# A retention block between two quantized FFNs: VectorE's first chains alternated, chunk 5's first FFN before V 0, and steps 2 and 3 in another order

## The chip, the cores and the metric

One Trainium2 chip, eight cores, one batch element per core: every core runs the same program on its own X of 2048 x 1024, with its own copy of all weights. The metric is the device time of the slowest core in microseconds.

## What is computed

For each X (fp32), with H = 8 heads of DH = 128:

```python
x = x + 0.5 * ffn(layernorm(x), W, b)      # "f1"
x = x + attn(layernorm(x))                 # retention: k q g v, sc, ret, wo
x = x + 0.5 * ffn(layernorm(x), W, b)      # "f2", the same W and b
# ffn: x and W quantized in blocks of 32 to the FP6 E2M3 grid, scaled back, x @ W.T + b
# attn: scores q k^T / sqrt(DH), causal, decayed by gamma_h^(n-m), times v;
#       normalised per head; silu(x @ W_G) * that, @ W_O
```

## The kernel before, in words

The sequence is cut into 16 chunks of 128 rows (partitions). For every chunk c the program runs: layernorm statistics (`st1` on VectorE, small terms `sm1` on GpSimd), the centred copy `xc1` (ScalarE), quantization `q1` on VectorE (a maximum over blocks of 32, a scale, a reciprocal, a multiply that writes fp8; it counts semaphore v_q1), scaling back `xd1` and the addition of the bias `b1` (GpSimd), a transpose of xd1, the matmuls `f1` and their addition into x, `ev1` (VectorE). Then `st2`, `sm2`, the normalised t (`tn`, ScalarE), its transpose, four projections `proj` k, q, g, v of 16 matmuls of 128 x 512 each, which are emptied by `evK`, `evQ`, `evG` (ScalarE) and `evV` (VectorE); the scores `sc`, `mask` (VectorE), `ret` with the update of the running state, `gn` statistics (VectorE), `smG` (GpSimd), `norm` (ScalarE), `zmul` (VectorE), the transpose of z, `wo`, `evO`. Then the second FFN with `st3`, `sm3`, `xc2`, `q2`, `xd2`, `b2`, `f2`, `ev2`, and a store.

At the start the FFN's weight is quantized in 8 blocks of 128 rows: `wquant` (lines 413 to 428, four steps, VectorE), `wy8` (rounding to fp8, ScalarE), `wd` (scaling back, GpSimd), a transpose `wtr` on TensorE and its copy `wcp` out of PSUM (ScalarE). A step on VectorE that needs the result of the step before waits for a semaphore of its own engine (`step`, line 409). The other weights come by `cast_load` (line 1039), fp32 to bf16, two halves each, issued from GpSimd. wg and wo have their place where the FFN's weight was staged, so they are loaded only when its blocks are through. Everything else is loaded by SyncE (`x_first`, line 280), which also issues the transposes by DMA: `xdt1` from chunk 6 on, `tt` from 3, `kt` and `qt` from 1, `zt`, `xdt2` (lines 293 to 333). The earlier ones go over TensorE (`turn`, line 903) and a copy on ScalarE (`turned`, line 706).

Each engine works through a list written out by hand: SyncE's is at lines 351 to 403, VectorE's at 534 to 635, ScalarE's at 723 to 811, TensorE's at 935 to 1029, GpSimd's at 1115 to 1207. The first four "steps" are irregular, and from chunk 4 (STEADY) on a loop repeats one pattern, in which f1 is three chunks ahead of the projections and f2 three behind. In each list an instruction that waits holds all behind it.

The matmuls write into three pairs of PSUM banks, P0 to P2; P1 also holds sc and ret. `psum_users` (line 86) lists, in TensorE's order, which work takes which pair, and `emptied` (line 824) makes each wait for the emptying of the last one: `EMPTIED`, line 120. v_sb, z_sb, st_sb, kt_sb and qt_sb are single buffers; `kt(c)` waits for the scores of c-1, `qt(c)` for ret of c-1, `evV(c)` for the state update of c-1.

Of the kernel before, what the change touches and what calls it, by code (L numbers as in the profile page):

```python
# [124 lines left out]
def build_program():  # L125
# [280 lines left out]
    def prog_vector(e):  # L406
# [126 lines left out]

        wquant(0)
        wquant(1)
        st1(0)
        for j in range(2, 6):
            wquant(j)
        q1(0)
        wquant(6)  # L540
        st1(1)
# [731 lines left out]
```

## Time and profile before

| | |
|---|---|
| Median of 3 runs | 484.29 us (484.23 to 484.36) |
| The profiled execution | 484.67 us, of which the slowest core's span is 482.8 us |
| The other cores' spans | 479.5 to 481.6 us |
| TensorE busy | 432.3 us (90%) |
| VectorE, ScalarE, GpSimd busy | 342.6, 190.5, 256.4 us |
| The chain that ended last | TensorE 72%, VectorE 12%, issue 6%, ScalarE 3%, DMA 3% |
| DMA engines' busy share, first tenths of the span (0 to 108 us) | 0.7, then 0.9 and more, until about 100 us |
| The last multiply of the weight's quantization ends | 40.9 us |
| x of 512 KB, median from issue to landing | 5.3 us |
| A halved weight by cast load, median to landing | wk 19.9, wq 31.5, wg 40.0, wv 41.2, wo 34.0 us |

Times in the rows are microseconds from the span's start of the slowest core. A busy share is the time in which an engine worked; matmuls are pipelined, so a busy TensorE is not at its peak. An idle time in brackets stands before the instruction and names what released it. What matters in this kernel is where TensorE stands idle, and which engine's list it then waits for.

### The profile page before, as it was taken

The page shows a single profiled execution, that of the slowest core. Times are in us where ns is not written, and L with a number is a line of the kernel's source. Part 1 is how long each engine was busy: PE and PEld are TensorE (multiplying, and loading weights), DVE is VectorE, ACT ScalarE, POOL GpSimd, SP SyncE. Part 2 cuts the span into 40 slices and gives each one's busy share as a digit, 9 for nine tenths or more (in the row PEclk, how much of TensorE's full clock was granted, in tenths as well). Part 3 has the DMA queues.
Part 4 walks back from the last instruction along what each step waited for, and adds up shares of the span by engine and source line. Part 5 has one row for each costly group of instructions (what it writes and reads, how often), then busy time and mean ns, then how long its engine had stood idle before and what let it go on. Part 6 is the DMA issues. An engine that isn't in the chain of part 4 may idle for free.

```text
span 482.8 us, 8182 instructions; the slowest of 8 cores (479.5 to 482.8 us)
## 1 busy us (share of the span) xinstructions
PE 432.3 (90%) x2410; PEld 215.5 (45%) x2456; DVE 342.6 (71%) x656; ACT 190.5 (39%) x270; POOL 256.4 (53%) x328
## 2 busy tenths in 40 slices
PE   0226799999998999999999999999999999999894
PEld 0113354545543535454545445454545454555442
DVE  3886866477888859687786868586947466756782
ACT  1547265236442071607061533426152534614400
POOL 0888765325477554655647464647451624436243
PEclk9999899999999999999999999999999999999999
DMA  7999999974363393635343533645340524233143
GB/s 200 309 182 182 189 157 183 155 116 87 89 110 67 94 208 92 110 67 143 75 133 67 153 68 88 88 88 88 87 81 12 107 45 85 47 67 65 44 153 131
DMA packets 99451, 54.47 MB, mean 113 GB/s; under 512 B 88784, under 2 KB 89040, under 8 KB 99408
## 3 DMA queue, kind: packets, MB, share of 16 engines
q1 hardware_dynamic: 93984, 43.43, 39.5%
q0 software_dynamic: 5280, 10.49, 14.9%
q8 instruction: 20, 0.33, 0.3%
q14 instruction: 23, 0.19, 0.1%
q10 hardware_dynamic: 144, 0.03, 0.0%
HBM read 34.28 MB, written 8.39 MB: 88 GB/s over the span
## 4 chain that ended last, share of the span: by engine, by line
PE 72%; DVE 12%; issue 6%; ACT 3%; DMA 3%; POOL 2%; SPq 1%; DVEq 1%; ACTq 0%; POOLq 0%
PE p L818 64%; DVE p L419 2%; DVE arena L434 2%; PE p L928 2%; DMA arena<-arena 2%; PE pstate L908 1%; PE p L859 1%; DVE arena L444 1%; DMA arena<-wf 1%; PE p L863 1%; PE p L847 1%; ACT arena L709 1%; ACT arena L681 1%; PE pstate L872 1%; DVE arena L522 1%
## 5 line engine op out<-in xcount | busy, mean ns | idle before, releaser
L818 PE MATMUL p<-arena 128*128 128x512 bf16 x1715 | 383.2, 379 | 8.1 <-ACT arena L709 2.7
L818 PEld LDWEIGHTS p<-arena 128*128 128x128 bf16 x1760 | 169.6, 98 | 206.8 <-issue 10.6
L434 DVE BATCH_NORM_STATS2 arena<-arena 128x6 f32<-128x512 f32 x96 | 66.5, 692 | 9.9 <-DVE arena L436 2.2
L669 ACT ACTIVATE arena<-arena 128x1024 bf16<-128x1024 f32 x16 | 19.9, 1243 | 129.1 <-POOL arena L1072 129.1
L1112 POOL TENSOR_TENSOR arena<-arena 128x1024 bf16<-128x1024 fp8e4 x16 | 34.3, 2144 | 46.9 <-DVE arena L449 46.9
L681 ACT ACTIVATE arena<-p,arena 128x128 bf16<-128x128 f32 x128 | 46.4, 473 | 19.2 <-POOL arena L1085 19.2
L444 DVE TENSOR_REDUCE arena<-arena 128x32 f32<-128x1024 f32 x29 | 35.3, 1216 | 19.3 <-ACT arena L660 10.8
L513 DVE TENSOR_TENSOR arena<-p,arena 128x1024 bf16<-128x1024 f32 x16 | 19.6, 1223 | 41.0 <-PE p L818 40.5
L908 PE MATMUL pstate<-arena 128*128 128x128 bf16 x168 | 16.4, 261 | 34.3 <-POOL arena L1048 27.5
L1105 POOL TENSOR_TENSOR arena<-arena 128x1024 bf16<-128x1024 fp8e4 x16 | 30.5, 1909 | 29.3 <-DVE arena L449 26.3
L449 DVE SCALAR_TENSOR_TENSOR arena<-arena 128x1024 fp8e4<-128x1024 f32 x29 | 37.3, 1285 | 3.4 <-DVE arena L448 0.5
L1091 POOL TENSOR_TENSOR arena<-arena 128x1024 f32<-128x1024 f32 x16 | 37.6, 2350 | 3.3 <-ACT arena L653 3.3
L1096 POOL TENSOR_TENSOR arena<-arena 128x1024 f32<-128x1024 f32 x16 | 37.5, 2346 | 0.0
L1052 POOL TENSOR_SCALAR arena<-arena 128x1 f32<-128x1 f32 x48 | 10.7, 224 | 44.6 <-DVE arena L436 43.1
L1082 POOL TENSOR_SCALAR arena<-arena 128x8 f32<-128x8 f32 x16 | 4.0, 250 | 53.8 <-DVE arena L526 53.8
L689 ACT CAST arena<-p 128x1024 bf16<-128x1024 f32 x16 | 16.2, 1014 | 41.1 <-PE p L818 41.1
L908 PEld LDWEIGHTS pstate<-arena 128*128 128x128 bf16 x168 | 13.5, 118 | 39.5 <-issue 38.4
L1053 POOL TENSOR_TENSOR arena<-arena 128x1 f32<-128x1 f32 x48 | 27.3, 570 | 7.1
L709 ACT COPY arena<-pstate 128x1024 bf16<-128x1024 bf16 x21 | 20.9, 1009 | 21.4 <-PE pstate L908 19.0
L503 DVE TENSOR_TENSOR arena<-p,arena 128x1024 bf16<-128x1024 f32 x16 | 19.5, 1220 | 13.2 <-PE p L847 12.9
L522 DVE BATCH_NORM_STATS2 arena<-p 128x6 f32<-128x128 f32 x128 | 26.8, 282 | 2.3 <-PE p L859 2.0
L1084 POOL TENSOR_TENSOR arena<-arena 128x8 f32<-128x8 f32 x16 | 26.8, 1676 | 2.3
(52 smaller groups left out, 397.1 us busy)
## 6 DMA issues: line engine op xcount, KB each, us to landing
arena<-x SPq DMA_DIRECT2D x16, 512.0 KB, 5.3
out<-arena SPq DMA_DIRECT2D x16, 512.0 KB, 2.8
arena<-wf SPq DMA_DIRECT2D x8, 512.0 KB, 11.5
arena<-wk POOLq DMA_DIRECT2D x2, 1024.0 KB, 19.9
arena<-wq POOLq DMA_DIRECT2D x2, 1024.0 KB, 31.5
arena<-wg POOLq DMA_DIRECT2D x2, 1024.0 KB, 40.0
arena<-wv POOLq DMA_DIRECT2D x2, 1024.0 KB, 41.2
arena<-wo POOLq DMA_DIRECT2D x2, 1024.0 KB, 34.0
```

The costliest lines, as they stand in the source:

```text
L434: step(e.bn_stats(bn_ln[:, n, 6 * half:6 * half + 6], x[:, 512 * half:512 * half + 512]))
L444: step(e.tensor_reduce(amax.unsqueeze(2), b32(xc), AX, ALU.max, apply_absolute_value=True))
L449: e.scalar_tensor_tensor(b32(y8), b32(xc), sm[:, n, c, 2:3], bc32(rs), ALU.mult, ALU.mult, saturate=False).then_inc(sem[done], 1)
L522: own.up(e.bn_stats(bn_gn[:, h, :], P1[:, h * 128:(h + 1) * 128]))
L681: e.activation(z_sb[:, h * 128:(h + 1) * 128], P1[:, h * 128:(h + 1) * 128], AF.Identity, scale=gn_a[:, h:h + 1], bias=gn_nb[:, h:h + 1]). ...
L818: last = e.matmul(pair[:, half * 512:half * 512 + 512], lhs[:, kc, :], w[:, kc, half * 512:half * 512 + 512], start=(kc == 0), stop=(kc == ...
L908: last = e.transpose(tb[n % 2][:, kc * 128:(kc + 1) * 128], src[:, kc * 128:(kc + 1) * 128], id_sb)
L1053: step(e.tensor_tensor(sm[:, n, c, 0:1], sm[:, n, c, 3:4], nhalf[:, 0:1], ALU.pow))
L1091: e.tensor_tensor(x_sb[c % XR], x_sb[c % XR], bias_sb, ALU.add).then_inc(sem["g_b1"], 1)
L1096: e.tensor_tensor(x_sb[c % XR], x_sb[c % XR], bias_sb, ALU.add).then_inc(sem["g_b2"], 1)
L1105: e.tensor_tensor(b32(xd1_sb[c % 2]), b32(y81_sb[c % 2]), bc32(q1_scl[c % 2]), ALU.mult).then_inc(sem["g_xd1"], 1)
L1112: e.tensor_tensor(b32(xd2_sb), b32(y82_sb), bc32(q2_scl), ALU.mult).then_inc(sem["g_xd2"], 1)
```

## The change

It touches the lists of all five engines and the list of PSUM users.

- VectorE: `wquant` and the first three `q1` and `st1` are split into single steps (w_max, w_scale, w_recip, w_mul; x_max, x_scale, x_recip, x_mul; x_st for each half, x_mean). They stand interleaved, so that most steps wait for one that lies two or more instructions back. The waits are on the count that its own forerunner reached. After them, st1(5) stands before q1(4), ev1(5) before evV(0), st2(3) before st1(6), evV(2) right behind gn(1), st1(7) behind st3(0).
- ScalarE: a small activation into `warm` before the first wy8, behind the same wait for g_const; wy8(1) before xc1(0); xc1(2) before wcp(7); xc1(5) before tn(2); xcp(5) before evG(1); xc1(6) behind evG(2) and evK(2) before norm(0); xc1(7) behind xc2(0), evQ(3) before scopy(2).
- TensorE: f1(1) in halves with the turn of x2 between them; xtr(5) before proj(1, "g"); f1(5) before proj(0, "v") instead of behind ret(0); proj(2, "g") before sc(1) and proj(2, "v") before ret(1); proj(3, "k") before f1(6) and proj(3, "q") before ret(2).
- GpSimd: the loads of wg's second half and wv's first are issued behind sm1(2); xd1(2) before b1(1); wv's second half behind sm2(0); sm1(5) before b1(4); sm2(3) before sm1(6); sm1(7) behind sm3(0).
- SyncE: kt(1) and qt(1) before the load of chunk 6, which waited for k 1; the load of chunk 7 waits for wv; kt(2) before zt(0); qt(3) before xdt2(0).

```diff
-             ("g", 1, 1), ("v", 0, 0), ("sc", 0, 1), ("v", 1, 2), ("ret", 0, 1),
-             ("f1", 5, 0), ("k", 2, 2), ("q", 2, 0), ("sc", 1, 1), ("g", 2, 2),
-             ("ret", 1, 1), ("wo", 0, 0), ("v", 2, 2),
-             ("f1", 6, 0), ("sc", 2, 1), ("k", 3, 2), ("ret", 2, 1), ("wo", 1, 0),
-             ("q", 3, 2), ("g", 3, 0), ("f2", 0, 2), ("v", 3, 1)]
+             ("g", 1, 1), ("f1", 5, 0), ("v", 0, 2), ("sc", 0, 1), ("v", 1, 0),
+             ("ret", 0, 1), ("k", 2, 2), ("q", 2, 0), ("g", 2, 2), ("sc", 1, 1),
+             ("v", 2, 0), ("ret", 1, 1), ("wo", 0, 2),
+             ("k", 3, 0), ("f1", 6, 2), ("sc", 2, 1), ("q", 3, 0), ("ret", 2, 1),
+             ("wo", 1, 2), ("g", 3, 0), ("f2", 0, 2), ("v", 3, 1)]
...
# SyncE
-        e.wait_ge(sem["t_k"], 2)
+
+        kt(1)
+        qt(1)
         x_first(6)
 
-        kt(1)
+        e.wait_ge(sem["ld_wv"], 32)
         x_first(7)
-        qt(1)
+        kt(2)
         zt(0)
         tt(3)
-        kt(2)
         qt(2)
...
         kt(3)
+        qt(3)
         xdt2(0)
         x_first(9)
-        qt(3)
...
# VectorE
+        def w_scale(j):
             if j >= 4:
                 e.wait_ge(sem["g_wd"], j - 3)
...
+            e.wait_ge(sem["v_self"], at["w_max", j])
+
+            own.up(e.tensor_scalar(w_scl[j % 4], w_amax[j % 4], 0.5 * R7_5, 0.5 * FLOOR,
+                                   ALU.mult, ALU.max))
+            at["w_scale", j] = own.n
...
+        w_max(0)
+        w_scale(0)
+        w_max(1)
+        w_recip(0)
+        w_scale(1)
+        w_mul(0)
+        x_st(0, 0)
+        w_recip(1)
+        x_st(0, 1)
+        w_mul(1)
+        w_max(2)
+        x_mean(0)
+        w_scale(2)
+        for j in range(3, 6):
+            w_max(j)
+            w_recip(j - 1)
+            w_scale(j)
+            w_mul(j - 1)
+        x_max(0)
+        w_recip(5)
+        x_scale(0)
+        w_mul(5)
+        w_max(6)
+        x_recip(0)
+        w_scale(6)
+        x_mul(0)
+        x_st(1, 0)
+        w_recip(6)
+        x_st(1, 1)
+        w_mul(6)
+        w_max(7)
+        x_mean(1)
+        w_scale(7)
+        x_st(2, 0)
+        w_recip(7)
+        w_mul(7)
+        x_max(1)
+        x_st(2, 1)
+        x_scale(1)
+        x_mean(2)
+        x_recip(1)
+        x_mul(1)
+        x_max(2)
+        x_scale(2)
+        x_recip(2)
+        x_mul(2)
...
         st1(4)
+        st1(5)
         q1(4)
         ev1(3)
-        st1(5)
         q1(5)
         ev1(4)
+        ev1(5)
         evV(0)
         mask(0)
 
         gn(0)
         evV(1)
+
+        st2(3)
         st1(6)
-
-        ev1(5)
-        st2(3)
         zmul(0)
         mask(1)
         q1(6)
-        st1(7)
         gn(1)
+        evV(2)
         evO(0)
         st3(0)
-        evV(2)
+        st1(7)
         zmul(1)
...
# TensorE
         f1_half(0, 1)
-        f1(1)
+        f1_half(1, 0)
         xtr(2)
+        f1_half(1, 1)
         f1_half(2, 0)
...
         f1(4)
+        xtr(5)
         proj(1, "g")
-        xtr(5)
         e.wait_ge(sem["s_t"], 3)
         turn("t2", t_sb)
+        f1(5)
         proj(0, "v")
 
         sc(0)
         proj(1, "v")
         ret(0)
 
-        f1(5)
         proj(2, "k")
         proj(2, "q")
+        proj(2, "g")
         sc(1)
-        proj(2, "g")
+        proj(2, "v")
         ret(1)
         wo(0)
-        proj(2, "v")
-
+
+        proj(3, "k")
         f1(6)
         sc(2)
-        proj(3, "k")
+        proj(3, "q")
         ret(2)
         wo(1)
-        proj(3, "q")
         proj(3, "g")
...
# GpSimd
         cast_load("wg", 0)
         wd(5)
-        cast_load("wg", 1)
         xd1(0)
         b1(0)
         wd(6)
-        cast_load("wv", 0)
         sm1(1)
         wd(7)
         xd1(1)
         sm1(2)
+        cast_load("wg", 1)
+        cast_load("wv", 0)
+        xd1(2)
         b1(1)
+        sm2(0)
         cast_load("wv", 1)
-        xd1(2)
-        sm2(0)
         b1(2)
```

ScalarE's part of the diff is told in the list above.

## Rows read from the trace of the kernel before

**Rows 1.** Table of windows: length, busy (instructions) of each engine, clock, DMA share, GB/s.

```profile
130.00:190.00 60.00, 56.77 (x321) 27.84 (x326) 50.15 (x92) 19.95 (x30) 36.08 (x43) 1.00 0.54 110
...
190.00:250.00 60.00, 59.69 (x321) 29.16 (x326) 46.65 (x103) 24.52 (x36) 33.41 (x49) 1.00 0.50 111
```

**Rows 2.** Timeline, VectorE, one weight block: start, duration, line, shapes.

```profile
15.60 1.23 DVE L419 TENSOR_REDUCE p<-arena 128x32 f32<-128x1024 f32 x1 [0.17 <-DVE arena L436]
...
16.93 0.19 DVE L422 TENSOR_SCALAR arena<-p 128x32 f32<-128x32 f32 x1
...
17.23 0.36 DVE L424 RECIPROCAL p<-arena 128x32 f32<-128x32 f32 x1
...
17.76 1.22 DVE L427 SCALAR_TENSOR_TENSOR arena<-arena,p 128x1024 f32<-128x1024 f32 x1 [0.17 <-DVE p L424]
...
18.90 1.22 DVE L419 TENSOR_REDUCE p<-arena 128x32 f32<-128x1024 f32 x1
```

**Rows 3.** Chain that ended last, 48 to 60 us: start, duration, what.

```profile
48.46 1.24 DVE p L444
...
50.69 1.29 DVE arena L449
...
52.19 1.91 POOL arena L1105
...
56.30 2.94 PE p L928 x8
...
59.24 0.85 PE pstate L908 x8
```

**Rows 4.** Timeline, GpSimd: sm1(2)'s first instruction, and b1(1).

```profile
46.63 0.21 POOL L1052 TENSOR_SCALAR arena<-arena 128x1 f32<-128x1 f32 x1
...
48.28 2.36 POOL L1091 TENSOR_TENSOR arena<-arena 128x1024 f32<-128x1024 f32 x1
```

**Rows 5.** Timeline, TensorE: sc(0), three projections, sc(1).

```profile
96.13 0.61 PE L847 MATMUL p<-arena 128*128 128x128 bf16 x8
...
101.14 10.36 PE L818 MATMUL p<-arena 128*128 128x512 bf16 x47
...
111.34 0.61 PE L847 MATMUL p<-arena 128*128 128x128 bf16 x8
```

**Rows 6.** DMA issues: KB each, us to landing; issued at 25.65, 32.24, 50.57, 98.23.

```profile
arena<-wq POOLq DMA_DIRECT2D x1, 1024.0 KB, 34.3
...
arena<-wg POOLq DMA_DIRECT2D x1, 1024.0 KB, 41.9
...
arena<-wv POOLq DMA_DIRECT2D x1, 1024.0 KB, 39.2
...
arena<-x SPq DMA_DIRECT2D x1, 512.0 KB, 6.2
```

**Rows 7.** Timeline: gn(0) to evV(1), q1(6) to st1(7) on VectorE; a ScalarE pass.

```profile
100.75 1.68 DVE L522 BATCH_NORM_STATS2 arena<-p 128x6 f32<-128x128 f32 x8 [1.99 <-PE p L859]
...
103.10 1.19 DVE L513 TENSOR_TENSOR arena<-p,arena 128x1024 bf16<-128x1024 f32 x1
...
113.27 1.21 DVE L444 TENSOR_REDUCE arena<-arena 128x32 f32<-128x1024 f32 x1
...
116.66 1.48 DVE L434 BATCH_NORM_STATS2 arena<-arena 128x6 f32<-128x512 f32 x2
...
118.60 1.15 ACT L653 ACTIVATE arena<-arena 128x1024 f32<-128x1024 f32 x1 [0.55 <-DVE arena L436]
```

**Rows 8.** Chain that ended last, 129 to 156 us.

```profile
129.11 1.21 DVE arena L503
...
137.18 1.12 DVE arena L484
...
150.91 4.70 DMA arena<-arena
...
155.84 2.32 PE p L818 x10
```

More of the change, by code:

```diff
@@ new lines, in x_max, with x_scale @@
+        def x_max(c):
+            e.wait_ge(sem["s_xc1"], c + 1)
+            own.up(e.tensor_reduce(x_amax[c].unsqueeze(2), b32(xc1_sb[c % 2]), AX, ALU.max,
+                                   apply_absolute_value=True))
+            at["x_max", c] = own.n
+        def x_scale(c):
+            e.wait_ge(sem["g_sm1"], c + 1)
+            if c >= 2:
+                e.wait_ge(sem["g_xd1"], c - 1)
+            e.wait_ge(sem["v_self"], at["x_max", c])
+            own.up(e.tensor_scalar(q1_scl[c % 2], x_amax[c], sm[:, 0, c, 1:2], FLOOR,
+                                   ALU.mult, ALU.max))
+            at["x_scale", c] = own.n
@@ new lines, in x_recip, with x_mul, x_st @@
+        def x_recip(c):
+            e.wait_ge(sem["v_self"], at["x_scale", c])
+            own.up(e.reciprocal(x_rs[c], q1_scl[c % 2]))
+            at["x_recip", c] = own.n
+        def x_mul(c):
+            e.wait_ge(sem["v_self"], at["x_recip", c])
+            e.scalar_tensor_tensor(b32(y81_sb[c % 2]), b32(xc1_sb[c % 2]),
+                                   sm[:, 0, c, 2:3], bc32(x_rs[c]), ALU.mult, ALU.mult,
+                                   saturate=False).then_inc(sem["v_q1"], 1)
+        def x_st(c, half):
+            if c >= 1 and half == 0:
+                e.wait_ge(sem["v_st1"], c)
+            e.wait_ge(sem["ld_x%d" % c], 16)
+            own.up(e.bn_stats(bn_ln[:, 0, 6 * half:6 * half + 6],
+                              x_sb[c][:, 512 * half:512 * half + 512]))
+            at["x_st", c] = own.n
@@ L531, in zmul @@
             e.tensor_tensor(z_sb, z_sb, g_sb[c % 2], ALU.mult).then_inc(sem["v_z"], 1)
[L534 to L541, printed above, removed]
-        wquant(7)
-        q1(1)
-        st1(2)
-        q1(2)
+        w_max(0)
[44 more added lines that the diff above has]
+        x_mul(2)
         ev1(0)
@@ L723, in prog_scalar @@
         e.dma_start(out=id_sb, in_=id_dr).then_inc(sem["ld_ident"], 16)
-        for j in range(KC - 1):
-            wy8(j)
-            if 2 <= j:
-                wcp(j - 2)
-            if j == 2:
-                xc1(0)
-            if j == 4:
-                e.wait_ge(sem["ld_bias"], 16)
-                e.activation(bias_sb, bias_sb, AF.Identity, scale=0.5
-                             ).then_inc(sem["s_bias"], 1)
-        xc1(1)
+        e.wait_ge(sem["g_const"], 2)
+        e.activation(warm, nhalf, AF.Identity, bias=ntie)
+        wy8(0)
+        wy8(1)
+        xc1(0)
+        for j in range(2, 6):
+            wy8(j)
+            wcp(j - 2)
+        e.wait_ge(sem["ld_bias"], 16)
+        e.activation(bias_sb, bias_sb, AF.Identity, scale=0.5).then_inc(sem["s_bias"], 1)
+        wcp(4)
+        wy8(6)
         wcp(5)
         xcp(0)
+        xc1(1)
         wy8(7)
         wcp(6)
+        xc1(2)
         wcp(7)
-        xc1(2)
         xcp(1)
@@ L754, in prog_scalar @@
         turned("q0", qt_sb)
+        xc1(5)
         tn(2)
@@ L766, in prog_scalar @@
         scopy(0)
+        evK(2)
         norm(0)
+        evQ(2)
+        tn(3)
+        evG(2)
         xc1(6)
-        evK(2)
-        tn(3)
-        evQ(2)
-        evG(2)
         scopy(1)
+        norm(1)
+        evK(3)
+        xc2(0)
         xc1(7)
-        norm(1)
-        xc2(0)
-        evK(3)
+        evQ(3)
         scopy(2)
-        evQ(3)
         norm(2)
@@ L1146, in prog_gpsimd @@
         sm2(1)
+        xd1(3)
         cast_load("wo", 0)
-        xd1(3)
+        b1(3)
         cast_load("wo", 1)
-        b1(3)
         sm1(4)
         sm2(2)
+        sm1(5)
         b1(4)
         xd1(4)
-        sm1(5)
         b1(5)
@@ L1159, in prog_gpsimd @@
         smG(0)
+        sm2(3)
         sm1(6)
         b1(6)
-        sm2(3)
         xd1(6)
-        sm1(7)
         smG(1)
         sm3(0)
+        sm1(7)
         b1(7)
```

43 lines of the change are left out of this document (23 added, 20 removed).

## The prediction

> **What bounds the kernel now.** I read the table of windows first, then the timeline of the start, then the chain of waits. From about 190 us on TensorE is full [rows 1]: its list of matmuls is the same in both kernels, so the change can only move the moment at which that gapless stretch begins. Between 130 and 190 us TensorE is idle for 3.2 us [rows 1], and the chain of waits says why: it runs over VectorE from the mask of chunk 2 (129.11) to the transposing DMA that feeds f2(1), where TensorE stands for 1.55 us at 155.84 [rows 8]. The next such point, f2(2) near 184 us, hangs on the same engine's list: ev2(1), gn(3), st2, st3. So there are two limits one behind the other: up to about 125 us the start (VectorE's quantization, then TensorE), from there to 184 us VectorE's list. In the start, VectorE works without a real pause, and in dependent pairs: each of the four steps of a weight block waits for the one before [rows 2]. The last of its products that TensorE needs is y8 of chunk 2 (50.69), from which xd1, the turn and f1(2) follow [rows 3].
>
> **VectorE's alternating chains.** One weight block takes 3.30 us from reduce to reduce: 1.33 + 0.30 + 0.53 + 1.14 [rows 2]. The last step, multiply to the next block's reduce, needs no result of its forerunner, and there the next instruction starts 0.08 us before the 1.22 us are over; at the dependent steps it starts 0.10 to 0.18 after. Alternated (reduce j, reciprocal j-1, scale j, multiply j-1) I get 1.15 + 0.28 + 0.18 + 1.14 = 2.75 us, 0.55 less. I stepped the new list through from 7.15 us with these intervals, and ScalarE and GpSimd beside it: multiply 0 ends at 11.4, multiply 2 at 18.3, 5 at 26.5, chunk 0's y8 at 29.4, multiply 7 at 35.7, where it ends at 40.9 now. GpSimd does not bind before: a block costs it 1.91 and an issue of a cast load 0.8, together 2.7 us, the same pace. ScalarE's table load goes off the path, but multiply 0 is 0.96 later since reduce 1 stands before it: 0.3 us gained.
> From here others set the pace. Chunk 1: xc1(1) ends at 36.2, its y8 at 40.3; GpSimd does wd(7) to 40.0, xd1(1) to 42.4, and only then sm1(2), 1.65 us [rows 4], to 44.1. Chunk 2's scale waits for that; multiply at 45.0, against 50.69 [rows 3]: 5.7 us earlier. xd1(2) goes in front of b1(1), turn at 48.5.
> The skill speaks against this part. The Trainium skill, VectorE: DVE Perf Modes, section "The DRAIN you can't avoid", says that the next operation starts when the pipe is empty and that a semaphore after each adds nothing; by it, alternation would save nothing. The trace disagrees: 1.14 against 1.33 us behind instructions of 1.22 [rows 2].
>
> **TensorE up to sc(0).** f1_half(0,1) and f1_half(1,0) fit in front of the turn of x2. f1_half(1,1) then covers ScalarE's copy, which stands open today until 56.30 [rows 3]. f1_half(2,0) took 2.94 us [rows 3]; eight matmuls at the later rate (0.217 each, [rows 5]) take 1.74. I take the faster for three of the four halves and the slow one where the 1.6 us before x2's turn hide it; if all run slow it costs 1 to 2 us. The next wait is t0: ev1(0) 46.7, st2(0) to 49.8, on GpSimd b1(1), 2.36 [rows 4], to 50.7, sm2(0) to 52.1, tn(0) to 53.5, turn at 53.6 where 59.04 is now (the first of the two turns that rows 3 merge at 59.24). After k 0 the turn of t1 waits another 0.7 us, since sm1(3) and b1(2) stand before sm2(1). Now from 59.04 to sc(0) at 96.13 [rows 5] are 37.1 us; less 0.4 for a wait before x4's turn and 0.6 for slow matmuls, plus the new wait 0.7, plus f1(5), 16 x 0.217 = 3.5. New sc(0): 53.6 + 40.3 = 93.9, call it 94.1. Against the same work now (96.13 + 3.5) it is 5.5 us earlier.
>
> **Loads.** The cast loads of the weights are one queue with a backlog: wg's second half lands 41.9 us after its issue at 32.2, wv's 39.2 after 50.6 [rows 6], so these two, with one load between them, land at 74.1 and 89.8, 7.8 apart each, though they were issued 18.4 apart. Issuing wg 1 at 44 instead leaves two loads before it unfinished, so I price it at nothing, and the landings stay. q 0 wants wq at 60.5 and it lands at 60.0 (34.3 after 25.7 [rows 6]); g 0 wants wg at 76.0, v 0 wants wv at 90.6. None waits, by 0.5, 1.9 and 0.8 us; chunk 5's earlier load shares the engines with the first, so up to 1 us stands against me there. That f1(5) stands before v 0 is what makes the second hold; without it v 0 would be ready at 87.1 and wait 2.7. Chunk 6's load now waits for kt(1) and qt(1): issued at 99.9 instead of 73.8. The load issued at 98.2 took 6.2 us [rows 6]; so 106, and st1(6) begins then rather than at 105. VectorE has 1.5 us to spare there. Bounds: nothing, and 1.5 us if it takes 9.
>
> **Step 2.** v 1, ret(0) with its state update, k 2, q 2, g 2: sc(1) at 109.4 (now 111.34 without g 2 [rows 5]; like for like 5.4 earlier). gn(0) takes 2.35 [rows 7], evV(1) is done at 102.1 before q 2 at 102.5. The queue of SyncE: kt(2) stands before zt(0) and waits for sc(1), so z 0's transpose starts at 111.1 and lands 3 to 4.7 later, wo(0) wants it at 114.6: 0 to 0.9, hidden by the next wait. On ScalarE xc1(6) is now behind evG(2): two passes, 1.15 us for the longer [rows 7], to 111.6. From there VectorE: q1(6) 3.39 [rows 7], gn(1) 2.35, evV(2) 1.2, end 118.7. k 3 takes the PSUM pair of v 2 and waits for evV(2): it starts at 118.8 instead of 118.2. k 3, f1(6): sc(2) at 125.8, mask(2) at 126.35. Now it is at 129.11 [rows 8]: 2.75 us earlier. So of 5.4 us half is given back, in the chain evG(2), xc1(6), q1(6), gn(1), evV(2), k 3, and because k 3 and f1(6) now both stand before sc(2).
>
> **Step 3 and the rest.** Behind mask(2) VectorE's list is unchanged: ev1(6), q2(0), gn(2) (ret(2) is over at 130.6, in time), evO(1). wo(1) ends at 134.5, so evO(1) starts at 134.6 against 137.18 [rows 8]: 2.5 left. st3(1), q1(7), zmul(2), q2(1) follow at their old pace, f2(1)'s transpose lands at 153.1 and f2(1) starts there. TensorE would be ready for f1(7) at 144.8 and stands 2.7 us for the transpose of xd1(7) and 1.9 before f2(1) instead: that is where its lead goes. qt(3) before xdt2(0) waits until 131 and hides no later than xd2(0) does. From f2(1) to f2(2) near 184 everything is VectorE's, ScalarE's and SyncE's old order, and behind it TensorE is full; tail and loads are the same. Sum: 2.5 us off the profiled execution, 484.67 to 482.2. The median of the runs lies 0.4 below that execution, at 484.29, so **481.8 us**.
>
> **Rivals.**
> (A) The forecast, 481.8, with 480.6 to 483.0 for 1 us either way in step 2.
> (B) The lead is kept. Were VectorE's list behind 129 us elastic (the gaps there are waits on a late TensorE, such as 1.4 us before zmul(1)), f2(1) would follow TensorE. For it: mask(2) is gated by sc(2). Against it: gn(2) to q2(1) stand back to back. A f2(1) right behind f1(7) and sc(3), at 148.8, would give 7 us; half of what lies between is 4.7: 479.6.
> (C) The start gains, the middle does not: the x6 load takes 9 us, the first halves run slow, or a weight lands 2 us late at q 0, g 0 or v 0. Each takes 1 to 2 us of the 2.5: 483.3 to 484.5, no change that can be told.
> (D) Slower. The new steps 2 and 3 pay only if sc(0) comes early: the path from sc(0) to mask(2) is 32.3 us, against 33.0 now with f1(5) in it (3.5), so 2.8 longer of its own, k 3 being in it. From sc(0) later than 96.8 mask(2) comes later than 129.1. If alternation saved nothing, multiply 7 stays at 41.7, chunk 2's y8 at 51, sc(0) at 99.6, mask(2) at 131.9: 2.8 us slower, 487.1. For it: nothing in the trace, where the small steps may yet have a floor that 1.14 does not show; half of the saving lost gives 484.4. This is also what the rule named above makes of it.
> A late cast load belongs here as a lesser form: if wg 1 landed 42 us after its issue instead of by its place in the queue, g 0 would wait 10 us. The even spacing speaks against it.
>
> **Chances.** A 0.56, B 0.14, C 0.19, D 0.11. Within 0.2% is within 1 us, which is about what a measurement of this kernel can tell from no change. Faster is A, B and a third of C: 0.77; same is most of C and a little of D: 0.13; slower 0.10. The range takes B and C in: 479.4 to 484.8.
>
> **What would show it.** Multiply to multiply of the weight blocks 2.75 us; y8 of chunk 2 at 45; turn of t0 near 53.6; sc(0) near 94; sc(1) near 109.4; mask(2) near 126.4; TensorE idle between 144 and 154 for 3 us or more in all; f2(1) near 153.3. A mask(2) at 129 or later, TensorE waiting on a cast load, or f2(1) before 152 makes it wrong.

## The result, and the profile after

| | before | after |
|---|---|---|
| Median of 4 runs each, one job | 484.26 us (484.20 to 484.36) | 487.21 us (486.87 to 487.45) |
| Ratio, 95% interval | | 1.0057 (1.004 to 1.0074) |
| Spans of the cores | 479.5 to 482.8 | 481.8 to 485.2 |

The change makes the kernel 2.9 us slower. Forecast were 481.8 us, a range up to 484.8 and a chance of 0.10 for slower: it was wrong. In some executions of the experiments below one die ran at a lower clock and some per cent longer; medians and ratios here leave these out.

The alternation itself does what it should. Timeline of VectorE, kernel after, core 3, beside [rows 2]:

```profile
16.28 1.22 DVE L421 TENSOR_REDUCE p<-arena 128x32 f32<-128x1024 f32 x1
17.41 0.35 DVE L436 RECIPROCAL p<-arena 128x32 f32<-128x32 f32 x1
17.67 0.17 DVE L430 TENSOR_SCALAR arena<-p 128x32 f32<-128x32 f32 x1
17.87 1.22 DVE L443 SCALAR_TENSOR_TENSOR arena<-arena,p 128x1024 f32<-128x1024 f32 x1
19.00 1.22 DVE L421 TENSOR_REDUCE p<-arena 128x32 f32<-128x1024 f32 x1
```

Reduce to reduce is 2.72 us where it was 3.30. The Trainium skill, VectorE: DVE Perf Modes, section "The DRAIN you can't avoid", says that the next operation does not start before the pipe is empty, and the prediction took from it that alternation would save nothing. But the same paragraph goes on to say that a next operation that is not held starts earlier. The rows, 1.13 us from a 1.22-us instruction to an independent next one, are in line with that second sentence.

What the forecast of the start left out are the loads. Reduce 1 now stands before multiply 0, so it wants the second weight block earlier. Timeline of VectorE, kernel after, first core 0, then core 3 (reduce 2, statistics of chunk 2, multiply 7):

```profile
7.98 1.23 DVE L421 TENSOR_REDUCE p<-arena 128x32 f32<-128x1024 f32 x1 [2.00 <-DMA arena<-wf]
```

```profile
14.84 1.23 DVE L421 TENSOR_REDUCE p<-arena 128x32 f32<-128x1024 f32 x1 [0.55 <-DMA arena<-wf]
...
35.39 0.69 DVE L477 BATCH_NORM_STATS2 arena<-arena 128x6 f32<-128x512 f32 x1 [0.62 <-DMA arena<-x]
...
36.45 1.22 DVE L443 SCALAR_TENSOR_TENSOR arena<-arena,p 128x1024 f32<-128x1024 f32 x1
```

Six of the eight cores wait 0.35 to 2.00 us for a weight block (wf), and core 3 another 0.95 for x; in the kernel before no core waits for either. Counted from the first reduce, multiply 7 ends at 29.9 us in the median of the cores and at 30.2 on core 3. It was 33.8 before, and 28.6 was forecast.

Behind the weight blocks VectorE waits for other engines. Before, it stood once there (core 2, reduce of chunk 2):

```profile
48.46 1.23 DVE L444 TENSOR_REDUCE p<-arena 128x32 f32<-128x1024 f32 x1 [2.39 <-ACT arena L653]
```

Now it stands three times. Timeline of VectorE, kernel after, core 3 (y8 of chunk 2, ev1(0); beside [rows 3]):

```profile
42.76 1.23 DVE L449 TENSOR_REDUCE p<-arena 128x32 f32<-128x1024 f32 x1 [1.34 <-ACT arena L738]
45.83 0.25 DVE L458 TENSOR_SCALAR arena<-p,arena 128x32 f32<-128x32 f32 x1 [1.84 <-POOL arena L1147]
46.18 0.36 DVE L464 RECIPROCAL p<-arena 128x32 f32<-128x32 f32 x1
46.66 1.28 DVE L469 SCALAR_TENSOR_TENSOR arena<-arena,p 128x1024 fp8e4<-128x1024 f32 x1
48.68 1.23 DVE L527 TENSOR_TENSOR arena<-p,arena 128x1024 f32<-128x1024 f32 x1 [0.74 <-PE p L1016]
```

Of the 3.4 us from 42.76 to 46.18, 1.84 are a wait for GpSimd's sum of chunk 2 (line 1147). TensorE in that stretch and at the points that answer to [rows 5] and [rows 8] (L1016 f1_half, L996 turns, L935 sc, L906 projections and f1):

```profile
44.88 6.19 PE L1016 MATMUL p<-arena 128*128 128x512 bf16 x16
50.91 0.61 PE L996 MATMUL pstate<-arena 128*128 128x128 bf16 x8
...
55.59 0.61 PE L996 MATMUL pstate<-arena 128*128 128x128 bf16 x8 [0.63 <-ACT arena L754]
...
96.91 0.61 PE L935 MATMUL p<-arena 128*128 128x128 bf16 x8
...
112.11 0.61 PE L935 MATMUL p<-arena 128*128 128x128 bf16 x8
...
122.45 7.07 PE L906 MATMUL p<-arena 128*128 128x512 bf16 x32 [1.10 <-DVE arena L566]
129.36 0.61 PE L935 MATMUL p<-arena 128*128 128x128 bf16 x8
...
151.33 5.30 PE L906 MATMUL p<-arena 128*128 128x512 bf16 x16 [2.75 <-DMA arena<-arena]
156.46 0.61 PE L935 MATMUL p<-arena 128*128 128x128 bf16 x8
156.91 3.62 PE L906 MATMUL p<-arena 128*128 128x512 bf16 x16
...
169.91 3.61 PE L906 MATMUL p<-arena 128*128 128x512 bf16 x16 [1.14 <-DVE arena L537]
```

Three things are to be seen. sc(0) starts at 96.91, hardly later than the 96.13 of [rows 5] though f1(5), 3.45 us, now stands before it: so the start did gain. From sc(0) to sc(2) it is 32.4 us, and it was 31.2: f1(5) is gone from that stretch, and yet it got longer, since k 3, as long as f1(5), moved in and waits 1.10 for evV(2) (line 566). And f1(7) (151.33) waits 2.75 us for its transpose, then takes 5.30 instead of 3.61, so that sc(3) comes at 156.46 where it was at 153.68. VectorE's mask(3) follows 2.3 us later than before, and at 169.91 TensorE waits for VectorE once more. Timeline of VectorE, mask(3) before (core 2), then mask(2) and mask(3) after (core 3; mask(2) before is in [rows 8]):

```profile
154.93 1.23 DVE L503 TENSOR_TENSOR arena<-p,arena 128x1024 bf16<-128x1024 f32 x1 [0.24 <-DVE arena L436]
```

```profile
130.14 1.23 DVE L556 TENSOR_TENSOR arena<-p,arena 128x1024 bf16<-128x1024 f32 x1 [1.40 <-PE p L935]
...
157.25 1.23 DVE L556 TENSOR_TENSOR arena<-p,arena 128x1024 bf16<-128x1024 f32 x1 [1.50 <-PE p L935]
```

The span ends 2.4 us later than before.

The table of windows shows the clock under it, and stands beside [rows 1]. From 190 us on TensorE is full in both kernels, as the forecast had it. After, core 3:

```profile
40.00:60.00 20.00, 16.41 (x92) 8.12 (x90) 12.97 (x19) 8.29 (x8) 16.30 (x21) 0.83 1.07 184
130.00:190.00 60.00, 55.21 (x305) 26.41 (x304) 49.20 (x89) 19.13 (x30) 37.98 (x42) 0.97 0.51 106
140.00:160.00 20.00, 17.25 (x79) 7.63 (x78) 16.64 (x23) 7.24 (x12) 15.97 (x18) 0.91 0.32 71
190.00:250.00 60.00, 60.00 (x335) 29.43 (x333) 47.58 (x102) 22.58 (x33) 32.38 (x46) 1.00 0.59 110
```

The granted clock (third number from the right) is 0.91 between 140 and 160 us; the kernel before had 1.00 there. In three of the eight cores (4, 5, 7) it stayed up: f1(7) took 3.61 and sc(2) to sc(3) 25.4 us, against 5.05 to 5.30 and 26.9 to 27.1 in the other five. So I count two stretches on every core: from its first reduce to sc(0), since the first weight block lands at 4.5 to 7.5 us, another time on each core and in each run, and from sc(0) to the span's end ("tail").

| Core median, us | before | after |
|---|---|---|
| First reduce to sc(0) | 87.6 (87.2 to 89.2) | 89.8, of which f1(5) 3.45 |
| sc(0) to sc(2) | 31.2 | 32.4 |
| sc(0) to mask(2) | 33.0 | 33.2 |
| sc(2) to sc(3) | 26.35 | 27.1, or 25.4 at full clock |
| mask(2) to mask(3) | 25.8 | 27.1, or 25.9 at full clock |
| mask(3) to the end | 327.9 | 327.9 |
| Tail | 386.6 | 388.0 to 388.3, or 387.0 to 387.1 |

The sum for the five cores with the slow f1(7): the start gains 1.3 (like for like, at the medians), f1(5) costs 3.45 ahead of sc(0) and nothing comes back for it behind (tail +0.4), and the clock costs 1.2 more. That is 3.8 us. The spans of the two slowest cores differ by 2.4 only, since the slowest one before, core 2, had a start 1.3 us over its kernel's median, and the slowest after, core 3, one 0.4 under it.

Two things follow. From mask(2) on all is as before: where the clock stays up, mask(3) and the end keep their distance from it to 0.1 us. And a block moved in front of sc(2) therefore has to be paid in full, unless something in front of mask(2) gets shorter by it; here sc(0) to mask(2) got 0.26 us longer although f1(5) left it.

### The profile page after: what moved, and what is told of

Same layout as the page of the kernel before. It is cut to its first block, busy times and chain, and to the rows that moved or that the text cites. A ratio compares the mean times of both kernels' runs of the same rounds, so it can differ in the third digit from the quotient of the medians.

```text
span 485.2 us, 8227 instructions; the slowest of 8 cores (481.8 to 485.2 us)
## 1 busy us (share of the span) xinstructions
PE 437.1 (90%) x2456; PEld 215.6 (44%) x2456; DVE 340.7 (70%) x656; ACT 191.1 (39%) x271; POOL 257.7 (53%) x328
## 4 chain that ended last, share of the span: by engine, by line
PE 67%; DVE 9%; DMA 6%; issue 6%; POOL 5%; ACT 3%; SPq 1%; DVEq 0%; POOLq 0%; ACTq 0%
PE p L906 62%; DMA arena<-x 6%; POOL arena L1194 2%; DVE arena L489 1%; PE p L935 1%; DVE arena L575 1%; DVE arena L501 1%; PE p L947 1%; ACT arena L766 1%; SPq L277 1%; PE p L951 1%; PE pstate L960 1%; POOL arena L1180 1%; DVE arena L527 1%; DVE arena L547 1%
## 5 line engine op out<-in xcount | busy, mean ns | idle before, releaser
L906 PE MATMUL p<-arena 128*128 128x512 bf16 x1744 | 386.0, 380 | 9.0 <-DMA arena<-arena 2.8
L906 PEld LDWEIGHTS p<-arena 128*128 128x128 bf16 x1744 | 168.6, 98 | 209.0 <-issue 15.8
L489 DVE BATCH_NORM_STATS2 arena<-arena 128x6 f32<-128x512 f32 x90 | 62.3, 693 | 11.4 <-DVE arena L491 2.7
L996 PE MATMUL pstate<-arena 128*128 128x128 bf16 x168 | 15.8, 253 | 32.1 <-POOL arena L1137 27.0
L1194 POOL TENSOR_TENSOR arena<-arena 128x1024 bf16<-128x1024 fp8e4 x16 | 30.5, 1909 | 26.0 <-DVE arena L506 24.5
L506 DVE SCALAR_TENSOR_TENSOR arena<-arena 128x1024 fp8e4<-128x1024 f32 x29 | 38.8, 1337 | 3.0
L794 ACT COPY arena<-pstate 128x1024 bf16<-128x1024 bf16 x21 | 21.0, 1008 | 26.9 <-PE pstate L996 20.5
L996 PEld LDWEIGHTS pstate<-arena 128*128 128x128 bf16 x168 | 12.7, 114 | 37.6 <-issue 36.2
L527 DVE TENSOR_TENSOR arena<-p,arena 128x1024 f32<-128x1024 f32 x16 | 19.5, 1218 | 12.9 <-PE p L906 11.9
## 6 DMA issues: line engine op xcount, KB each, us to landing
arena<-wf SPq DMA_DIRECT2D x8, 512.0 KB, 12.9
arena<-wg POOLq DMA_DIRECT2D x2, 1024.0 KB, 32.4
```

The lines of the kernel that those rows point to most:

```text
L489: step(e.bn_stats(bn_ln[:, n, 6 * half:6 * half + 6], x[:, 512 * half:512 * half + 512]))
L506: e.scalar_tensor_tensor(b32(y8), b32(xc), sm[:, n, c, 2:3], bc32(rs), ALU.mult, ALU.mult, saturate=False).then_inc(sem[done], 1)
L906: last = e.matmul(pair[:, half * 512:half * 512 + 512], lhs[:, kc, :], w[:, kc, half * 512:half * 512 + 512], start=(kc == 0), stop=(kc == ...
L996: last = e.transpose(tb[n % 2][:, kc * 128:(kc + 1) * 128], src[:, kc * 128:(kc + 1) * 128], id_sb)
L1194: e.tensor_tensor(b32(xd1_sb[c % 2]), b32(y81_sb[c % 2]), bc32(q1_scl[c % 2]), ALU.mult).then_inc(sem["g_xd1"], 1)
```

## The experiments

Fourteen experiments ran, each timed beside the kernel before in the same job. Diffs are against the kernel after where nothing else is said. "Start" is the first reduce to sc(0), "tail" sc(0) to the end of the span, both as core medians.

**1. The new start alone.** The new lists up to the projections, and everything from f1(5) on as before:

```diff
         proj(1, "g")
-        f1(5)
         proj(0, "v")
         sc(0)
         proj(1, "v")
         ret(0)
+        f1(5)
...
```

The rest of steps 2 and 3 is as in the kernel before, on all engines.

> The changed kernel's start (alternated VectorE chains, ScalarE's, TensorE's and GpSimd's start up to chunk 4) with the old order of everything behind it: f1(5) behind ret(0), steps 2 and 3, SyncE's list and the PSUM users as before. If the new order of steps 2 and 3 is what costs: sc(0) at 93.4 to 94, or at 94 to 95 if v 0 has to wait for wv; the old path of 33.0 us from sc(0) to mask(2) gives mask(2) near 127, and the end 2 to 2.5 us under the kernel before, about 482. If instead a lead of TensorE cannot pass VectorE's list or the loads, the end is within 1 us of the kernel before although sc(0) is 2.7 us earlier.

Measured: 482.52 against 484.66, ratio 0.996 (0.9934 to 0.9987). Start 86.0, tail 386.8. So the new start is worth 2.1 us, and its whole lead lasts: f1(7) waits 0.2 us at most, where the kernel after has the 2.75.

**2. The new order alone**, with the old start:

```diff
-        w_max(0)
-        w_scale(0)
...
+        wquant(0)
+        wquant(1)
...
```

f1(5) and steps 2 and 3 are as in the kernel after, on all engines.

> The old start with the new order behind it (f1(5) before v 0, steps 2 and 3, SyncE's list, PSUM users). If the new order costs what the path from sc(0) to mask(2) says (33.2 us in the changed kernel's trace, with f1(5) outside, against 33.0 with it inside): sc(0) near 99.7, mask(2) near 133, the end 4 to 6 us over the kernel before, 488 to 490. If the order costs only by TensorE's slower clock behind its wait at f1(7): 1 to 2 us over.

Measured: 489.83, ratio 1.010 (1.007 to 1.0131). On all eight cores f1(7) waits 2.7 us and then takes 5.30. By the ratios the order costs 4.8 us and the start brings 1.9; together that is, to 0.2 us, the 2.8 that the change costs. The core medians say the same of the order: start 91.2, 3.5 longer than before, and tail 388.0, 1.3 longer.

**3. The clock.** Twelve matmuls without use are put into f1(7)'s wait. Their results are overwritten by f1(7).

```diff
+FILL_AT = 7
+FILL_N = 12
...
+            if c == FILL_AT:
+                pair = emptied("f1", c)
+                for kc in range(FILL_N):
+                    e.matmul(pair[:, 0:512], wdt_sb[:, kc % KC, 0:128],
+                             wdt_sb[:, kc % KC, 0:512], start=True, stop=True,
+                             skip_group_check=True)
```

> The changed kernel, with 12 extra matmuls into the PSUM pair of f1(7) just before TensorE waits for chunk 7's transpose (2.6 us of filling where it stood for 2.75). If the granted clock of 0.5 behind that wait is part of the loss: f1(7) takes 3.6 us instead of 5.3, mask(3) and all behind it come 1.6 earlier, the end 1 to 2 us under the changed kernel, about 485.5. If VectorE's list sets the pace there anyway: no more than 0.3 us under it.

Measured: 486.91, ratio 1.0047 (1.0027 to 1.0067). On all eight cores f1(7) now takes 3.61 and sc(2) to sc(3) 25.4 us. Timeline of TensorE, core 3 of this kernel (L926 the added matmuls, L908 f1(7)):

```profile
149.23 2.75 PE L926 MATMUL p<-arena 128*128 128x512 bf16 x12
152.11 3.61 PE L908 MATMUL p<-arena 128*128 128x512 bf16 x16
155.56 0.61 PE L943 MATMUL p<-arena 128*128 128x128 bf16 x8
```

The median tail falls by 1.0 us to 387.1 (387.0 to 387.4): without the idle time before it f1(7) is not slow. In the time this can't be told: the ratio was 1.0057 without the matmuls, and the intervals overlap.

**4. evV(2) in front of gn(1)**, so that k 3 does not wait:

```diff
+        evV(2)
         gn(1)
-        evV(2)
```

> The changed kernel, with evV(2) in front of gn(1) on VectorE. If k 3's wait for evV(2) is on the path: k 3 starts behind wo(0) at 121.3 instead of 122.45, sc(2) 1.1 earlier, the end 0.8 to 1.1 us under the changed kernel, about 486.2. If gn(1), then smG(1) and norm(1), 1.2 us later, hold sc(2) (it needs P1 emptied by norm(1)), the gain is 0 to 0.3 us.

Measured: 487.63, ratio 1.0089 (1.0057 to 1.0122). sc(1) to sc(2) falls by 0.97 to 16.28 us, and f1(7) waits as long as before (2.7 to 2.9 us). Of the 0.97, 0.6 to 0.9 are lost again between mask(2) and mask(3) on the cores where f1(7) is not slow, and 0.1 to 0.4 of the tail is gained there: k 3's wait costs little of its own. On core 3 f1(7) took 3.61 behind an idle time of 2.93, on core 0 4.98 behind 2.91: an idle time of this length lowers the clock on some cores only.

**5 and 6. The start taken apart.** Run 5 is the kernel before with VectorE's alternation alone, run 6 is run 1 with the old dependent steps on VectorE.

```diff
-        wquant(0)
-        wquant(1)
+        w_max(0)
+        w_scale(0)
+        w_max(1)
...
```

This is run 5's, on the kernel before; run 6 is the reverse, on run 1.

> The kernel before with VectorE's alternated chains alone; every other engine's list is the old one. If alternation makes the start's gain: the median over the cores of sc(0) falls from 94.6 to about 92.7, the end is 1.5 to 2.3 us under the kernel before. If the loads and GpSimd's list (b1(1) before xd1(2)) hold chunk 2 anyway: less than 0.7 us under it.

> The kernel of e1_start with VectorE's old, dependent list at the start, all other engines' starts being the new ones. If alternation makes the gain: sc(0)'s median stays at 94 to 94.6 and the end within 0.5 us of the kernel before. If the other lists (xd1(2) before b1(1), f1(1) in halves, the table load) make it: the end is 1 us or more under the kernel before.

Measured: run 5 484.45, ratio 0.9989 (0.9973 to 1.0005), start 88.3; run 6 484.86, ratio 0.9999 (0.9981 to 1.0016), start 88.9. Neither alone brings anything that can be measured; together 2 us (run 1). In run 5 VectorE, now ahead, waits 3.94 us for GpSimd's sm1(1) and 3.24 for ScalarE's xc1(2) (core 1; 3.5 to 4.0 and 3.0 to 3.4 over all). The other engines' lists have to follow, or the wait only changes its name.

**7. k 3 behind sc(2)**, with the PSUM pairs of f1(6) and k 3 exchanged, the rest as after:

```diff
-        proj(3, "k")
         f1(6)
         sc(2)
+        proj(3, "k")
         proj(3, "q")
```

> The changed kernel with k 3 behind sc(2) again: f1(6), sc(2), k 3, q 3, ret(2), and the PSUM pairs of f1(6) and k 3 exchanged. The theory is that the end follows mask(2) at a fixed distance, since VectorE's list behind it has no room, so work moved in front of sc(2) is lost. Then f1(6) starts at 124.2 (chunk 6's transpose lands) instead of 125.9, sc(2) about 1.7 earlier in relation to sc(0), f1(7) as much, and the end 1.5 to 2.5 us under the changed kernel, 484.7 to 485.7. If instead TensorE's order does not matter there, sc(3) in relation to sc(0) and the end stay.

Measured: 492.54, ratio 1.0158 (1.0126 to 1.0189). A miss. sc(0) to sc(2) stays at 32.4 in the median (30.9 to 32.6), for f1(6) now waits 3.0 to 3.2 us for chunk 6's transpose, and sc(2) to sc(3) grows to 30.5, since ret(2) and wo(1) come later while ScalarE's list has evK(3) in front of xc2(0).

**8. f1(5) before v 0 with the old steps 2 and 3**, on run 1, chunk 5's small steps pulled forward with it:

```diff
+        f1(5)
         proj(0, "v")
         sc(0)
         proj(1, "v")
         ret(0)
-        f1(5)
```

> The kernel of e1_start with chunk 5's first FFN in front of v 0 and what belongs to it (turn of x5, st1(5), ev1(5), xc1(5), sm1(5) earlier), steps 2 and 3 as before. If f1(5)'s place alone costs nothing, sc(0) is 3.5 later, sc(0) to mask(2) 3.5 shorter, and the end is that of e1_start, about 2.1 us under the kernel before. If the waits that it brings (turn of x4, 0.4 us) stay on the path: 0.4 to 1 us more than e1_start.

Measured: 487.72, ratio 1.0061 (1.0039 to 1.0082). sc(0) to sc(1) falls from 15.2 to 12.9, not by f1(5)'s whole 3.45, with waits of 1.0 for norm(0) and 1.3 for evK(2) behind it. All of it is lost again behind sc(1): sc(1) to sc(2) grows from 15.9 to 18.8, and the tail of 388.0 to 389.2 (median 388.4) is 1.7 longer than run 1's.

**9. The reverse: f1(5) behind ret(0) again, new steps 2 and 3.**

```diff
-        f1(5)
         proj(0, "v")
         sc(0)
         proj(1, "v")
         ret(0)
+        f1(5)
```

ev1(5) goes back behind evV(1) with it.

> The changed kernel with f1(5) behind ret(0) again and the rest of its order of steps 2 and 3 kept. Theory 1: the end follows mask(2), and what counts is how many blocks of 16 matmuls stand before sc(2); there it makes no difference on which side of sc(0) f1(5) stands, so sc(0) is 3.5 us earlier (median near 92.4), sc(0) to sc(2) 3.5 longer, and the end that of the changed kernel less the 1.1 us of k 3's wait at most: 486 to 487. Theory 2: between sc(0) and sc(3) the other engines' chains set the pace and f1(5) filled a hole; then sc(0) to sc(3) stays at 58 and the end is near 484.

Measured: 487.36, ratio 1.0068 (1.0049 to 1.0086). sc(0) to sc(2) is 35.9, 3.5 longer than after, start 3.4 shorter, and the end is the same. With the new order f1(5)'s place is neutral. That leaves k 3: one block more between ret(0) and sc(2), and one fewer between sc(2) and f1(7). Against run 1 (31.1) sc(0) to sc(2) is 4.8 longer by it, and the tail 4.9 (391.6 against 386.8).

**10. The slow matmuls at 45 us.** 48 small matmuls of the identity, their results unused, behind the turns of w6 and w7 in run 1.

```diff
         wtr(6)
+        warm_up(14)
         wtr(7)
+        warm_up(34)
```

> The kernel of e1_start with 48 small extra matmuls (128 x 128 on the identity, into a PSUM pair not yet in use) in TensorE's gaps behind the turns of w6 and w7, so that it does not stand idle there. If the slower halves of f1(0) and f1(1) hold chunk 0's chain: these take 3.5 us instead of 4.6 to 6.2, the turn of t0 and sc(0) come 0.5 to 1.5 us earlier, the end as much under e1_start. If GpSimd's b1(1) in front of sm2(0) holds t0 anyway: sc(0) moves by less than 0.3 us, the end is e1_start's.

Measured: 482.97, ratio 0.9969 (0.9951 to 0.9987). The two halves at 45 us now take 3.62 on every core, where run 1's took 3.62 to 5.95, and yet sc(0) comes no earlier: the turn of x2 behind them waits 2.2 us for GpSimd. In run 1 the slow halves hide behind that.

**11. Chunk 6 freed** (its load, st1, xc1, sm1 and q1 earlier), step 3 on TensorE in the old order:

```diff
-        proj(3, "k")
         f1(6)
         sc(2)
-        proj(3, "q")
+        proj(3, "k")
         ret(2)
         wo(1)
+        proj(3, "q")
...
```

Moved with it are x_first(6) before kt(1), st1(6) before st2(3), xc1(6) behind norm(0), q1(6) before mask(1) and sm1(6) on GpSimd.

> The changed kernel, f1(5) still before v 0, with chunk 6 freed: its load at the old place (behind k 1), st1(6) before st2(3), xc1(6) right behind norm(0), q1(6) before mask(1), and in step 3 the old order f1(6), sc(2), k 3, ret(2), wo(1), q 3. If what costs is the chain evG(2), xc1(6), q1(6), evV(2), k 3 in front of sc(2): sc(0) to sc(2) falls from 32.45 to 28 to 29.5 us, mask(2) comes 3 to 4 earlier, and the end is 2.5 to 3.5 us under the changed kernel, 483.5 to 484.7. If f1(5) before v 0 costs by itself (the chain v 0, ret(0), norm(0) has a length of its own), sc(0) to sc(2) stays above 31 and the end above 486.

Measured: 488.68, ratio 1.0092 (1.0073 to 1.0111). sc(0) to sc(2) does fall to 29.5, at the upper end of what was expected. But sc(2) to sc(3) is 30.7: ScalarE's list has evK(3), which waits for k 3, in front of xc2(0), so that q2(0) and evO(1) come late, and g 3 waits 2.1 to 3.0 us for evO(1).

**12. The same with the old lists of step 3 on ScalarE, SyncE, VectorE and GpSimd too** (evV(2) stays behind gn(1)):

```diff
+        xc1(7)
         norm(1)
+        xc2(0)
 
         evK(3)
-        xc2(0)
-        xc1(7)
+        scopy(2)
         evQ(3)
-        scopy(2)
...
```

Besides, qt(3) comes behind x_first(9), st1(7) before gn(1), sm1(7) before smG(1).

> The kernel of the run on chunk 6, with step 3 given back its old lists on ScalarE (the last chunk's evictions and norm(1) first, xc2(0) ahead of k 3's eviction), on SyncE and on GpSimd; only step 2 keeps an order of its own. If the new order loses because the engines' lists lean on each other (the theory that the run on chunk 6 left): the interval from the scores of block 0 to those of block 2 stays at 29.3 us, the next one falls from 30.6 back to about 26.4, the tail behind the scores of block 0 is about 384.8 us, and the kernel ends at 482.5 to 483.5, as early as the new start with the old order or just ahead of it. If the tail is held by something else than the lists (k 3 in front of the scores of block 2 as such, chunk 7's products behind it): the third interval stays at 28 or more and the time at 485 or more.

Measured: 486.82, ratio 1.0043 (1.0026 to 1.006), start 89.8, tail 386.5. The time is that of the second expectation, the interval lies between the two: sc(2) to sc(3) fell from 30.7 to 27.2, so the lists were most of it, and sc(0) to sc(2) is 29.85. mask(2) comes 2.6 us sooner behind sc(0) than in the kernel after, but mask(3) stands 27.7 us behind it where the kernel after needs 25.9 at full clock, so 1.8 of the 2.6 are lost. But the tail is the tail of the kernel before, though it holds one block of 3.45 us less. The windows of run 12 (core 4) and then run 1 (core 6), each from sc(0) to sc(4), show where that block is:

```profile
sum 85.96, PE 80.45 PEld 39.03 DVE 68.69 ACT 35.84 POOL 49.53; mean PE 20.11 PEld 9.76 DVE 17.17 ACT 8.96 POOL 12.38
```

```profile
sum 86.41, PE 83.72 PEld 40.68 DVE 68.92 ACT 35.83 POOL 48.80; mean PE 20.93 PEld 10.17 DVE 17.23 ACT 8.96 POOL 12.20
```

TensorE is busy 3.3 us less and the stretch is 0.5 us shorter. VectorE's work in it is the same to 0.2 us. f1(5), taken out of this stretch, leaves idle time there, and in front of sc(0), where TensorE was the limit, it costs its whole length. I read it so that VectorE, GpSimd and ScalarE set the pace from sc(0) to sc(4); nothing was taken off them to show it. Runs 8, 9 and 12 together say more: with f1(5) in front of v 0 and k 3 behind sc(2) (487.72 and 486.82), or the other way round (487.36), the loss is about that of both moves together (487.21).

**13 and 14. The rest of the start's gain.** Run 13 is run 1 with GpSimd's sum for chunk 2 in front of xd1(1) (the first hunk). Run 14 adds, on TensorE, chunk 0's second half of f1 in front of the turn of x1 (the second).

```diff
+        sm1(2)
         xd1(1)
-        sm1(2)
...
         wtr(7)
+        f1_half(0, 1)
         xtr(1)
-        f1_half(0, 1)
         f1_half(1, 0)
```

> The new start with the old order behind it (the fastest so far, 482.5), with GpSimd's sum for chunk 2 moved ahead of its multiply for the turn of x1. If chunk 2's scale waits for GpSimd's list (it waited about 2 us there): its multiply starts at 44.3 instead of 46.25, the scores of block 0 come 1 to 1.9 us earlier, and the time is 0.5 to 1.5 us under that run. If the turn of x1 or GpSimd's b1(1) holds what stands behind it: the scores of block 0 and the time stay where they were, within 0.4 us.

> The kernel of the run before this one (GpSimd's sum for chunk 2 first) with chunk 0's second half of the first FFN in front of the turn of x1 on TensorE. There chunk 2's scale no longer waits, but VectorE's ev1(0) does, 3.0 to 3.6 us for that half, which stood behind the turn of x1 (43.8) and ran slowly. If that is what holds the start now: ev1(0) follows y8(2)'s multiply at 45 to 46.5, 1.5 to 2 us earlier, the turn of t0 comes at 53.4 or so as predicted at first, the scores of block 0 1 to 1.5 us earlier, and the time falls to 480.6 to 481.4. If GpSimd's b1(1) before its sum for t0 holds instead, or the matmuls stay slow: within 0.5 us of the run before, 482.1.

Measured: run 13 482.07, ratio 0.9959 (0.9943 to 0.9975), start 86.2, no gain at sc(0). The 2-us wait was gone, and VectorE waited elsewhere. Timeline of VectorE, run 13, core 0:

```profile
43.54 1.28 DVE L468 SCALAR_TENSOR_TENSOR arena<-arena,p 128x1024 fp8e4<-128x1024 f32 x1
48.44 1.22 DVE L526 TENSOR_TENSOR arena<-p,arena 128x1024 f32<-128x1024 f32 x1 [3.62 <-PE p L1015]
```

Run 14: 481.63, ratio 0.9948 (0.993 to 0.9966), start 85.6. The same steps on core 3 of run 14:

```profile
43.02 1.28 DVE L468 SCALAR_TENSOR_TENSOR arena<-arena,p 128x1024 fp8e4<-128x1024 f32 x1
45.51 1.23 DVE L526 TENSOR_TENSOR arena<-p,arena 128x1024 f32<-128x1024 f32 x1 [1.21 <-PE p L1015]
```

Its three quickest cores take 84.4 to 84.5 us to sc(0), where run 1's take 85.4 to 85.7, and their tails are 386.7 to 386.9. The cast loads are the next limit: on four cores v 0 waits 0.66 to 2.66 us. Core 2 took 89.2, for it waited on two of them (TensorE, timeline, run 14, core 2; q 0 and v 0):

```profile
61.66 3.61 PE L905 MATMUL p<-arena 128*128 128x512 bf16 x16 [0.85 <-DMA arena<-wq]
...
91.34 5.09 PE L905 MATMUL p<-arena 128*128 128x512 bf16 x16 [2.66 <-DMA arena<-wv]
```

Run 14 is the fastest kernel of the study. Its interval overlaps that of runs 1 and 13, so that it beats them is likely from the traces, not shown by the times.

## Why the prediction was wrong, point by point

- **VectorE's alternating chains: right.** 2.75 us per block forecast, 2.72 measured.
- **The start: mechanism right, its size the largest term that failed.** Forecast was a gain of 5.5 us at sc(0), like for like; by the core medians it is 1.3 after and 1.7 in run 1, and on the profiled cores (first reduce to sc(0), 89.0 and then 89.4 with f1(5) in it) 3.0. The first cause: I compared one core with itself. The profiled core 2 needed 89.0 us where the kernel's median is 87.6. The second: the loads of the weight blocks and of x were not in the sum, and multiply 7 ended 1.6 us late on core 3 (counted from the first reduce), 1.5 of it waits for loads. Chunk 2's multiply, forecast at 45.0, came at 46.66, 1.3 late by the same count, with the wait for GpSimd in front of it, and the two halves of f1 took 6.19 us instead of 4.7, so the turns came at 50.9 and 55.6 instead of 48.5 and 53.6. The third: from the turn of t0 to sc(0) TensorE took 41.3 us instead of 40.5. The sum took 0.4 off for a wait before x4's turn in the kernel before; between 59.04 and 96.13 that trace has no such wait, and the kernel after has one of 0.44 there. Also, VectorE did not work "without a real pause": the 2.39 us in front of 48.46 were one. Runs 13 and 14 shortened the waits for GpSimd and TensorE and won 0.4 us of the start at the medians, 1 us on the three quickest cores.
- **TensorE up to sc(1): right in its length.** 15.3 us forecast, 15.2 measured. The cast loads held TensorE up nowhere in the kernel after, as forecast. That v 0 would wait 2.7 us for its load if f1(5) did not stand before it shows in run 14, by 2.66 on core 2 and less or nothing on the others.
- **Step 2: sc(0) to mask(2) priced too low.** It was forecast at 32.3 us and took 33.2 on every core (mask(2) at 130.14, forecast 126.35; 2.8 of these 3.8 us are sc(0)'s own delay). evV(2) cost k 3 a wait of 1.10 instead of 0.6, since q1(6)'s scale took 0.97 instead of 0.24 (last section). Chunk 6's load cost VectorE 0.90 us at 107.67, which was slack, as forecast.
- **Step 3: right up to the wait, wrong on its price.** f1(7)'s wait was forecast at 2.7 and is 2.75, and VectorE's list behind mask(2) is as tight as was said. That the 16 matmuls behind the wait would take 5.30 was not in the sum, nor that mask(3) then comes 1.2 us later still. Worth 1.0 us of the tail (run 3).
- **The two sides of the sum.** Forecast: 5.5 us from the start against 2.8 for the order (the longer path of rival (D)), so 2.5 to 2.7 faster. Measured by runs 1 and 2: 1.9 against 4.8, so 2.9 slower. The start was put 3.6 too high. The order was put 2.0 too low: 0.9 of it in sc(0) to mask(2) and 1.1 in the clock. Run 2 shows the order to be the whole loss, and run 12 that it does not pay even with its lists mended.
- **Rival (B), a VectorE list that is elastic behind mask(2),** did not come: mask(2) to mask(3) is 25.8 us before and 25.9 after at full clock. It is a different thing that a lead which moves everything is kept, as in run 1 (1.7 us at sc(0), tail as before) and on the three quickest cores of run 14 (3.1 to 3.3 us under the median before).
- **Rival (D)** gave 487.1 and a break-even at sc(0) = 96.8. That the number came out is luck. Its condition was met (sc(0) at 96.91, mask(2) 1.0 us later than before), but by its own arithmetic this sc(0) costs 0.1 us, the rest came from sc(0) to mask(2) and from the clock, and alternation did save. It had 0.11 because I bound it to that one cause. The break-even itself stood only 2.7 us from the forecast, and the terms of the start could eat that.

## What to carry to other kernels

Where the limit changes hands along the run (here TensorE up to sc(0), the other engines' chain from there to sc(4), TensorE again), ask of each moved block which stretch it leaves and which it enters: moved into the stretch where its engine is the limit it costs its whole length, and what it gives back depends on what limits the stretch that it leaves. f1(5) out of the middle gave back nothing in run 12, and its whole 3.45 us only where k 3 had filled the middle before (run 9 against the kernel after). Forecast against the medians of all cores, each from its first data, and look for the break-even first: where the slack to it is smaller than the sum of the unknowns, the slower side deserves more than a tenth. Lists written by hand are one object: the six experiments that left the order behind ret(0) alone were not slower than the kernel before, and the eight that touched it, or put f1(5) ahead of it, all were.
